# Rotary step of a causal attention: the cosine product reads PSUM, batches are unrolled, the token copy for the values goes

## The reference

```python
q = jnp.einsum('btm,mhd->bthd', x, w_aq)      # k, v in the same way
q = _rope(q); k = _rope(k)
s = jnp.einsum('bihd,bjhd->bhij', q, k) / D_HEAD
s = s - INF_APPROX * mask                     # mask: i < j
p = jax.nn.softmax(s, axis=-1)
o = jnp.einsum('bhij,bjhd->bihd', p, v)
r = jnp.einsum('bihd,hdm->bim', o, w_ao)
# _rope: even, odd = split(x, 2, axis=-1)
#        concatenate([even * cos - odd * sin, even * sin + odd * cos])
```

## Time and profile before

| | |
|---|---|
| median of 3 runs | 1098.11 us (1096.88 to 1100.96) |
| span of the profiled execution | 1099.5 us (its own time is not listed apart from the span) |
| TensorE busy | 1008.7 us, 92% |
| VectorE busy | 890.4 us, 81% |
| ScalarE busy | 657.7 us, 60% |
| GpSimd busy | 598.5 us, 54% |
| end of the attention, start of the feed-forward part | about 808 us |

### The profile page before, as it was taken

How to read it: one execution, slowest core, us unless ns; L and a number is a source line. 1 busy time by engine, 2 the same in 40 slices (tenths; PEclk the granted TensorE clock), 3 DMA queues, 4 the chain that set the end, 5 groups by cost and what they waited for, 6 DMA issues and landing times. The chain is left out here.

```text
span 1099.5 us, 20887 instructions
## 1 busy us (share of the span) xinstructions
PE 1008.7 (92%) x5648; PEld 837.4 (76%) x5648; DVE 890.4 (81%) x1803; ACT 657.7 (60%) x1383; POOL 598.5 (54%) x536
## 2 busy tenths in 40 slices
PE   2699999999999999999999999999939999999995
PEld 1588787877878787887878788788727878788784
DVE  4888898989988899998889999898855758576744
ACT  4476776767776676777767777676625252252531
POOL 3667767777777778777777877777540100000000
PEclk8799999999999999999999999999978999999998
DMA  8542222732223242222223122222020000000000
GB/s 281 164 134 49 58 72 63 218 86 57 57 50 74 58 114 86 57 57 61 64 67 105 48 57 58 67 64 60 1 78 1 1 1 20 1 19 0 1 20 19
DMA packets 33838, 69.99 MB, mean 64 GB/s; under 512 B 5520, under 2 KB 7056, under 8 KB 32272
## 3 DMA queue, kind: packets, MB, share of 16 engines
q1 hardware_dynamic: 30976, 62.81, 21.4%
q10 hardware_dynamic: 2832, 6.82, 1.7%
HBM read 24.26 MB, written 7.34 MB: 29 GB/s over the span
## 5 line engine op out<-in xcount | busy, mean ns | idle before, releaser
L737 POOL TENSOR_SCALAR probs<-probs,inv_sum 128x128 f32<-128x128 f32 (+7 forms) x256 | 237.6, 928 | 178.5 <-DVE inv_sum L653 178.5
L554 ACT ACTIVATE pT<-psum 128x512 fp32r<-128x512 f32 (+3 forms) x384 | 176.7, 490 | 146.9 <-PE psum L420 144.7
L310 PE MATMUL psum<-pT,vals 128*128 128x512 f32 (+3 forms) x1152 | 246.9, 355 | 1.6 <-DVE rT L695 1.6
L542 ACT ACTIVATE probs<-psum,neg_max 128x128 f32<-128x128 f32 (+7 forms) x256 | 190.5, 744 | 52.5 <-DVE neg_max L647 49.0
L663 DVE TENSOR_TENSOR pT<-psum,pT 128x512 fp32r<-128x512 f32 (+3 forms) x384 | 199.8, 547 | 15.7 <-ACT pT L554 12.6
L310 PEld LDWEIGHTS psum<-pT,vals 128*128 128x128 f32 x1152 | 191.8, 193 | 24.1 <-DVE pT L663 1.7
L647 DVE TENSOR_REDUCE neg_max<-psum 128x1 f32<-128x128 f32 (+7 forms) x256 | 190.9, 746 | 11.0 <-PE psum L411 10.9
L420 PE MATMUL psum<-ident,probs 128*128 128x128 f32 x1152 | 178.5, 281 | 21.9 <-DVE pT L663 15.4
L742 POOL TENSOR_TENSOR swapped<-swapped,rope 128x512 f32<-128x512 f32 x128 | 165.4, 1292 | 40.5 <-DMA swapped<-proj 40.4
L749 POOL TENSOR_TENSOR qk<-swapped,qk 128x512 fp32r<-128x512 f32 x128 | 179.4, 1402 | 3.6 <-ACT qk L574 3.6
L918 PE MATMUL ps<-hid,w 128*128 128x512 f32 x768 | 181.3, 396 | 0.0
(11 more groups left out here) (78 smaller groups left out, 1241.7 us busy)
## 6 DMA issues: line engine op xcount, KB each, us to landing
swapped<-proj SPq DMA_DIRECT2D x256, 128.0 KB, 2.3
w_stage<-qk_split SPq DMA_DIRECT2D x30, 256.0 KB, 2.7
x_static<-x_moving SPq DMA_DIRECT2D x4, 1024.0 KB, 5.0
wv_stage<-v_split SPq DMA_DIRECT2D x15, 256.0 KB, 2.6
x_split<-ffn_raw ACTq DMA_DIRECT2D x2, 1024.0 KB, 5.9
ffn_raw<-g SPq DMA_DIRECT2D x2, 1024.0 KB, 8.0
x_moving<-x_split SPq DMA_DIRECT2D x2, 1024.0 KB, 4.9
out<-y SPq DMA_DIRECT2D x4, 512.0 KB, 2.6
```

What stands on the lines that cost most here:

```text
L310: ins = nc.tensor.matmul(out_ap, left[a], right[b], start=first and i == 0, stop=last and i == 2)
L542: nc.scalar.activation(probs[:, ib % 4, :width].rearrange("p (h c) -> p h c", h=halves), score_ps[:, ib % 2, :halves, :half], ACT.Exp, bia ...
L554: nc.scalar.activation(pT[chunk][:, 0, 4 * f:4 * f + n_blocks, (ib % 4) * P:(ib % 4 + 1) * P], bank("t", head[1], nth)[:, :n_blocks * P].r ...
L737: nc.gpsimd.tensor_scalar(p, p, inv_sum[:, n:n + 1], 1.0, ALU.mult, ALU.mult).then_inc(probs_ready[0], 1)
```

## The change

Three things change.

1. **The cosine product.** It reads the projection from its bank in PSUM and no longer from ScalarE's copy. It still waits for that copy, so that the two don't read the bank together. Its steps become those of the projection, `COS_STEP` = (0, 0, 2, 2), and its place in a step of VectorE moves from the head to just ahead of the values' low part. `by_cos` has four buffers in place of two. A projection's bank is released by the product (`cos_done`) and not by the copy, and the copy no longer waits for an earlier product.
2. **Batches are unrolled.** `run_pairs` writes, for each of the four batches, its first pair straight and a loop over the others (three rounds, two in the last batch, whose last pair is straight again). SP's program has its batches written out as well.
3. **No token copy.** The value projection takes its weights from `x_moving`. `x_static`, its four transfers and `x_fixed` are gone; the load of the next batch's tokens waits for the value projection of the last pair that used that half.

```diff
-COS_STEP = (1, 2, 3, 4)
+COS_STEP = (0, 0, 2, 2)
...
-    x_static = sb("x_static", [P, 2, T], F32R)
-    by_cos = sb("by_cos", [P, 2, BANK])
+    by_cos = sb("by_cos", [P, NQK, BANK])
...
-        steps(0, body)
-        with eng.Fori(1, PAIRS - 1) as pair:
-            steps(pair, body)
-        steps(PAIRS - 1, body)
+        for b in range(B):
+            steps(b, 0, body)
+            with eng.Fori(1, PAIRS_OF - (b == B - 1)) as hp:
+                steps(b, hp, body)
+        steps(B - 1, PAIRS_OF - 1, body)
...
-                    signal = {"t": t_low, "qk": proj_copied, "s": exp_done}[kind]
+                    signal = {"t": t_low, "qk": cos_done, "s": exp_done}[kind]
...
-                sp.wait_ge(qk_projected[0], NQK * H * (b - 1))
-                sp.wait_ge(x_fixed, 16 * b)
-                sp.dma_start(dst.bitcast(F32), src).then_inc(x_moved, 16)
+                wait_for_pair(sp, v_projected, PAIRS_OF * (b - 1) - 1, NV - 1)
+                sp.dma_start(x_moving[:, b % 2].bitcast(F32), x_split[b - 2]).then_inc(x_moved, 16)
...
-                        sp.dma_start(x_static[:].bitcast(F32), x_half.bitcast(F32)).then_inc(x_fixed, 16)
...
-                    pe.wait_ge(x_fixed, 16 * (2 * pair // H) + 16)
...
-                                          [x_static[:, part, t0:t0 + P] for part in range(2)],
+                                          [x_moving[:, b % 2, part, t0:t0 + P] for part in range(2)],
...
-                wait_for(act, cos_done, old_head, old)
...
-                wait_for(dve, rope_done, *earlier(head, j, 2, NQK))
-                nc.vector.tensor_tensor(by_cos[:, j % 2], proj[:, j % 2], rope[:, 0, c * BANK:(c + 1) * BANK],
+                wait_for(dve, rope_done, step_on(head, -1), j)
+                nc.vector.tensor_tensor(by_cos[:, j], bank("qk", 1 if parity(head) else 2, j),
+                                        rope[:, 0, c * BANK:(c + 1) * BANK],
                                         ALU.mult).then_inc(cos_done[0], 1)
...
-                for target, j in rope_tasks(head, s, COS_STEP):
-                    times_cos(target, j)
                 if exists(step_on(head, (s + 1) // NI)):
...
                 if exists(head):
                     transposed_low(head, s)
+                for target, j in rope_tasks(head, s, COS_STEP):
+                    times_cos(target, j)
                 for c in v_tasks(head, s):
                     values_low(head[0], c)
```

54 lines of the change are left out of this document (21 added, 33 removed).

## The result

| | before | changed |
|---|---|---|
| median, us | 1097.86 (1096.88 to 1100.96) | 1079.16 (1077.29 to 1084.27) |
| ratio to before | | 0.983, 95% interval 0.981 to 0.986 |
| span of the profiled run, us | 1099.5 | 1082.5 |

A forecast was written before the change was run, and what follows sets the result against it. TensorE was taken as the bound, its waits ended by VectorE's reciprocal and GpSimd's packed run; -9.0 (30 heads) - 1.1 (start) = -10.1 us from 1098.11 gave 1088.0 us, own range 1084 to 1092, wide range 1078 to 1099.

The forecast's parts named there:

- The product's form and cost: VectorE's cosine product, reading PSUM and SBUF, takes 0.68 us and nothing of it blocks GpSimd.
- Which of the two wins: GpSimd's low part meets VectorE's sum: run 0.36 us shorter if VectorE wins, 0.46 if GpSimd does; 0.40 taken.
- The reciprocal later by 0.10: Two products ahead of VectorE's 640-wide reciprocal delay it, and GpSimd's packed run, by 0.10 to 0.26 us; 0.10 taken.
- The sum per head: GpSimd's run ends 0.40 - 0.10 = 0.30 us earlier in either head; 30 heads give 9.0 us.
- The marks it named: Signs if right: TensorE's wait on L663 gone, the one on L749 longer, one to 1.2 us; a pair at 46.8.
- The start: In the prelude the third product, 1.77 us beside GpSimd, takes 0.68 in a chain TensorE waits for: 1.1 us gained.
- The clock: Rival: shorter idle time keeps TensorE's clock up, another 4 x 1.58 = 6.3 us go, 1082 us; chance 0.15.
- wide range: Total time of 1078 to 1099 us, leaving out the slower rival and the tail of the clock's.
- Hidden anyway: Rival: later reciprocal cancels the shorter packed run, or another wait holds the run; 1094 to 1098 us; chance 0.25.
- slower: Rival: GpSimd still stretches the product, the pair ahead of the reciprocal takes 2.2 us; 1117 us; chance 0.10.
- Unrolling and the token copy at nothing: Straight batches taken at 0 (bounds -3 and +8 us), the dropped token copy at nothing (bounds 0 and -0.5 us).
- The later bank release at nothing: Odd head's bank 1, released near 403.0 instead of 402.29, is wanted at 403.92: slack 0.9 us, so no cost.

The follow-up runs named there:

- e2_cos_only: Kernel before with only the cosine product's change (source, place, bank release) and three by_cos buffers: 1079.68 us, ratio 0.9821 to before.
- e4_copy_new_place: Changed kernel with the cosine product at its new place but reading ScalarE's copy in SBUF: 1096.1 us, ratio 0.997 to before.
- e10_run_longer: Changed kernel with GpSimd normalising the odd head's 640-wide and 768-wide blocks in two pieces each: 1095.27 us, ratio 0.9981 to before.
- e5_tile3_step3: Changed kernel with tile 3's cosine product at the end of step 3 instead of step 2: 1069.86 us, ratio 0.9725 to before.

## Why the prediction was right, and where it was short

**The product's form and cost: right.** Forecast 0.68 us, unaffected by GpSimd; measured mean 0.684.

**Which of the two wins: right in form, at the other of its two ends.** The forecast had 2.72 us for the low part and the 768-wide block together if VectorE wins, 2.62 if GpSimd does, and took a gain of 0.40. Measured are 1.30 and 1.35: GpSimd wins, and the run is 0.44 us shorter.

The meeting at 405.95, which I let pull the value down, was no accident, but of another kind. From 84 to 765 us the 512-wide block takes 1.23 us beside a sum of 0.69 at 28 of 29 places in before and at 26 of 29 in the changed kernel (350.43 and 350.48 are such rows). At the other places it comes out the other way, though the sum starts 0.05 to 0.06 us behind as always. `e2_cos_only` has six of them; the timelines of GpSimd and VectorE at one:

```profile
346.79 0.70 POOL L736 TENSOR_SCALAR probs<-probs,inv_sum 128x512 f32<-128x512 f32 x1
```

```profile
346.85 1.18 DVE L676 TENSOR_TENSOR swapped<-by_cos,swapped 128x512 f32<-128x512 f32 x1 [1.26 <-POOL swapped L741]
```

Here GpSimd keeps its free 0.70 and VectorE's sum is stretched, and with it the reciprocals behind it come later: the head takes 24.06 us in place of 23.62. The changed kernel has three such heads, each some 0.5 us longer, one reason why its median pair, 46.68, isn't its undisturbed one. Who wins a meeting this close is thus not fixed by the order of the two starts; what decides it is open.

**The reciprocal later by 0.10: right.** The pair of products takes the forecast's 1.20 us, start to start.

**The sum per head: a term that was mis-sized.** Forecast 0.30 a head, 0.60 a pair; measured 0.80 a pair. With 0.44 for the run it would have been 0.44 - 0.10 = 0.34 a head, and the odd head did gain that (23.94 to 23.60 us). The even one gained 0.42 (23.45 to 23.03), with the whole of its wait of 0.37 us gone. The prediction says there that TensorE waits for GpSimd instead and gains "about 0.30 and not its whole idle time"; it gained all of it. The marks it named were also wrong in part: the wait on the low part L663 did not go but shrank from 0.54 to 0.17, and the one on L749 stayed at 0.69 and didn't grow to 1. The forecast took VectorE's lag out of the odd head altogether; its subtraction still ends a wait there. Over 14 pairs this term is 11.2 us and not 8.4.

**The start: mis-sized.** Forecast 1.1 us for the third product; measured 1.9 at the first wide scores and 4.2 by the third head. The step counted one operation of the prelude and left out the clock: from 20 to 76 us before loses 11.9 us to it and the changed kernel 8.6.

**The clock: given as a rival, and it happened in good part.** It had a chance of 0.15 and 6.3 us; between the profiled spans 5.1 us of lost clock went in the steady part (6.8 to 1.7). The counter-argument, that 1.2 of 1.5 us stay, was true (1.16) and yet the falls went: no steady pair with 1.16 us had one. The kernels with a longer run show the same from the other side. This is the largest part of what was missing. The forecast put it at nothing, and that the time is still in the wide range is owed to that range's lower end, which let part of this rival in, and not to the sum. Added up between the profiled spans: 5.1 us of clock, 2.8 of the pairs and 3.1 of the start are 11.0, the three pairs with late swaps take 4.0 back, and 17.0 - 10.1 = 6.9 were to be found.

**Hidden anyway, slower.** Neither happened. The slower one is real where its condition holds (`e4_copy_new_place`).

**Unrolling and the token copy at nothing: right**, 1.0017 (1.0002 to 1.0031). The term's upper bound had +1 us for each entry into a loop, and the late swaps are of that kind: in the profiled run they lengthen the first round of three batches' loops by 0.7 to 1.5 us. Waits for a swap of 1 us or more are in the steady part of neither the kernel before nor `e2_cos_only`, which aren't unrolled, but in that of seven of the ten unrolled ones, most often in the first round of the second batch's loop. The page's instruction queues move 29 and 31 packets in place of 14 and 16; no run here ties these to the late swaps, whose cause stays open.

**The later bank release at nothing: right only together with the place.** With the product early the bank is free in time; with the product at its old place TensorE waits 0.58 us for it.

## What to carry to other kernels

When one engine's packed run sets the end, price an edit by that run's start and length. Here TensorE followed GpSimd's run nearly one for one in both directions (0.49 us of run, 0.48 of pair in `e10_run_longer`; 0.60 us ahead of it, 0.56 of odd head in `e5_tile3_step3`), but only in a head where it had a wait left to lose. Then look whether the waits form a cluster behind which the clock falls, since a few tenths there can cost or return as much again. And look at what an operation that gained from leaving a shared resource still stands ahead of: one product moved from before the reciprocal gave another 9.3 us.

## What the runs showed of the hardware that was not expected

- A low part moved behind another, with no operation longer, cost 16.5 us, most of it in the clock: 11.8 us lost at seven places where the changed kernel has 1.7 at one.
- When GpSimd's low part starts 0.11 to 0.13 us before VectorE's sum, the price moves and doesn't vanish: 1.30 and 1.72 us (free 1.27 and 0.69), and the 768-wide block behind takes 1.35.
- When GpSimd's 512-wide normalisation starts 0.05 to 0.06 us before that sum, there are two outcomes, with no difference to be seen in the starts: mostly 1.23 and 0.69 us, sometimes 0.70 and 1.18. In the changed kernel the second makes the head some 0.5 us longer.
- A VectorE operation that reads one operand from PSUM beside GpSimd isn't stretched (mean of 684 ns over 116), though the same one from SBUF has a mean of 992.
